# Gated cross-attention with experts: block 0's first chunks between the last attention turns, and the gate in two halves

## The reference, cut to what matters

```python
def reference(x, ctx_1024, mask_BxSxS2_bk1, g_xattn, g_ffn, ...):
    # x, ctx: (32, 128, 128) float32; 16 heads of 8; 8 experts, hidden width 512
    x = x + jnp.tanh(g_xattn[0]) * attention(_layernorm(x), ctx_1024, ctx_1024, mask, Wq, bq, ..., Wo, bo)
    x = x + jnp.tanh(g_ffn[0]) * ffn(_layernorm(x), Wg, bg, Wt, bt, W1, b1, W2, b2)
    return x

def ffn(inputs, ...):
    x = inputs.reshape(-1, 128)                        # 4096 tokens
    gate = jax.nn.softmax(x @ Wg + bg, axis=-1)        # 8 experts
    thr = jax.nn.sigmoid(x @ Wt + bt) * 0.125
    adapted = gate - thr
    w = adapted * (adapted >= 0)
    s = jnp.sum(w, axis=-1, keepdims=True)
    w = w / jnp.where(s == 0, 1, s)
    h = jax.nn.gelu(jnp.einsum('td,edf->etf', x, W1) + b1[:, None, :])   # every expert on every token
    eo = jnp.einsum('etf,efd->etd', h, W2) + b2[:, None, :]
    return jnp.einsum('te,etd->td', w, eo).reshape(inputs.shape)
```

## Time and profile before

| | us |
|---|---|
| three runs: median (lowest to highest) | 647.18 (643.64 to 647.93) |
| profiled execution: its own time | 640.58 |
| its span in the profile | 638.7 |
| TensorE busy in it | 596.9 |
| VectorE / ScalarE / POOL busy | 483.0 / 376.8 / 175.1 |
| mean granted clock of TensorE | 0.975 of full |

### The profile page before, as it was taken

One profiled execution on the slowest core, in us unless ns is written; L12 is line 12 of the kernel. 1 busy time (PEld: TensorE's weight loads), 2 busy tenths in 40 slices (PEclk: granted clock), 3 DMA queues, 4 the chain that ended last, 5 costly groups with the idle time before them and its releaser, 6 DMA issues.

```text
span 638.7 us, 13719 instructions
## 1 busy us (share of the span) xinstructions
PE 596.9 (93%) x4482; PEld 451.5 (71%) x4482; DVE 483.0 (76%) x926; ACT 376.8 (59%) x620; POOL 175.1 (27%) x223
## 2 busy tenths in 40 slices
PE   7688999999999986499999999999999999999998
PEld 5455666666666654478788788788787887887886
DVE  5467677777777764468888788888888888888886
ACT  2144555555555454277677667666676666666663
POOL 5433344544342331002212212112212112121121
PEclk9799899999999999599999999999999999999999
DMA  5955555656544510041121121121121121111210
GB/s 145 247 167 169 141 138 141 176 163 161 174 129 124 151 23 2 3 89 45 40 67 50 50 63 46 41 66 49 49 58 43 47 66 49 44 58 46 63 52 16
DMA packets 43966, 55.12 MB, mean 86 GB/s; under 512 B 9488, under 2 KB 27792, under 8 KB 42384
## 3 DMA queue, kind: packets, MB, share of 16 engines
q1 hardware_dynamic: 43472, 53.99, 30.2%
q10 hardware_dynamic: 448, 0.53, 0.3%
HBM read 39.16 MB, written 14.81 MB: 84 GB/s over the span
## 4 chain that ended last, share of the span: by engine, by line
PE 82%; DVE 5%; DMA 4%; ACT 4%; SPq 3%; issue 2%; ACTq 0%; POOL 0%; DVEq 0%
PE ps_h L1087 9%; PE ps_y L1067 9%; PE ps_y L1069 9%; PE ps_y L1068 9%; PE ps_h L1089 9%; PE ps_h L1088 9%; PE misc L931 4%; PE scores L869 4%; PE scores L897 3%; DMA kq_st<-maxT 3%; PE scores L909 3%; PE scores L886 3%; ACT probs L532 2%; PE misc L1035 1%; PE misc L957 1%
## 5 line engine op out<-in xcount | busy, mean ns | idle before, releaser
L616 ACT ACTIVATE h_sb<-ps_h,b_sb 128x512 f32<-128x512 f32 x256 | 176.2, 689 | 108.7 <-PE ps_h L1089 95.4
L820 DVE TENSOR_TENSOR h_low<-h_sb,h_high 128x512 fp32r<-128x512 f32 x256 | 164.3, 682 | 0.0
L495 POOL TENSOR_TENSOR yT<-yT,weighted 128x512 f32<-128x512 f32 x54 | 69.6, 1289 | 301.5 <-DVE weighted L808 301.5
L816 DVE CAST h_high<-h_sb 128x512 fp32r<-128x512 f32 x128 | 98.5, 770 | 68.1 <-ACT h_sb L616 68.1
L646 DVE TENSOR_REDUCE neg_max<-scores 128x8 f32<-128x1024 f32 x64 | 77.9, 1221 | 43.6 <-PE scores L869 43.6
L1087 PE MATMUL ps_h<-x_high,w_high 128*128 (+1 forms) x256 | 102.9, 402 | 1.7 <-ACT h_sb L616 1.7
L1067 PE MATMUL ps_y<-h_high,w_high 128*128 128x512 f32 x256 | 101.3, 396 | 0.6 <-DVE h_low L820 0.6
L1069 PE MATMUL ps_y<-h_high,w_low 128*128 128x512 f32 x256 | 101.2, 395 | 0.0
L1068 PE MATMUL ps_y<-h_low,w_high 128*128 128x512 f32 x256 | 101.2, 395 | 0.0
L1089 PE MATMUL ps_h<-x_high,w_low 128*128 (+1 forms) x256 | 100.8, 394 | 0.0
L1088 PE MATMUL ps_h<-x_low,w_high 128*128 (+1 forms) x256 | 100.3, 392 | 0.0
(11 more groups left out here) (124 smaller groups left out, 710.3 us busy)
## 6 DMA issues: line engine op xcount, KB each, us to landing
w_row<-w_scratch SPq DMA_DIRECT2D x64, 256.0 KB, 3.1
kq_st<-kq_scratch SPq DMA_DIRECT2D x64, 192.0 KB
kq_scratch<-kq_parts SPq DMA_DIRECT2D x30, 256.0 KB, 3.2
w_raw<-in_w_ffn SPq DMA_DIRECT2D x16, 256.0 KB, 3.3
kq_scratch<-kq_parts SPq DMA_DIRECT2D x32, 128.0 KB, 3.3
ctx_sb<-in_ctx SPq DMA_DIRECT2D x16, 128.0 KB, 2.6
out_y<-y_out SPq DMA_DIRECT2D x7, 256.0 KB, 2.3
x_all<-in_x SPq DMA_DIRECT2D x13, 128.0 KB, 2.2
```

What stands on the lines that cost most here:

```text
L616: nc.scalar.activation(h_sb[:, j % HBUF, :], ps_h[:, j % 4, :], ACT.Gelu_apprx_tanh, bias=b1_sb[:, j:j + 1]).then_inc(h_done, 1)
L816: V.tensor_copy(h_high[:, j % HBUF, :], h_sb[:, j % HBUF, :]).then_inc(high_odd, 1)
L820: V.tensor_tensor(h_low[:, j % HBUF, :], h_sb[:, j % HBUF, :], h_high[:, j % HBUF, :].bitcast(F32), ALU.subtract).then_inc(low2_done, 1)
```

## The change

It writes the same computation in another order.

- Block 0's chunks 0 to 7 (first halves) and 0 to 3 (second halves) go, on all three engines, between the steps of turns 16 to 19. The helpers `first`, `second`, `hidden`, `high`, `low` are taken out of the block bodies for it; block 0's body starts at chunk 8 (TensorE, ScalarE) or pair 6 (VectorE).
- ScalarE loads the Gelu table in turn 16 (`ready_gelu`, a Gelu of two columns), behind the last exponentials.
- The gate is split by tokens. Half 0 (blocks 0 to 3): steps 1 and 2, 3 to 7, 8 to 11, 12 to 15 stand behind the logits of turns 12, 13, 14 and 15 on VectorE, `gate_exps(0)` in turn 13 on ScalarE, `turn_gate(0)` in turn 17 on TensorE, `gate_copy(0)` in turn 17 on ScalarE. Half 1: steps inside block 1 of the expert stage, at pairs 0 and 2 one each, from pair 12 to 24 two each (the last has one), `gate_exps(1)` behind chunk 6, `turn_gate(1)` behind chunk 28, `gate_copy(1)` behind chunk 30. Each half is stored to DRAM by itself, the second behind block 1's loads of `w_row`.
- PSUM: `ps_y` changes places with `ps_t`, so that `ps_h` and `ps_y` lie over `scores` and only `ps_t` over `misc`; `expert_wT` goes to the end of the second stage's buffers.

TensorE, before: from the last turned maxima (`max_parts`, turn 15) to the first expert matmul. `x2n` is turned for x2T, `wg_sb` are logits, `ps_t<-ident_sb,g_exp` is the gate's turn.

The diff, cut to its core (waits and helpers as they are where not shown):

```diff
+            def gate_exps(half):
+                ts = slice(B // 2 * half, B // 2 * (half + 1))
+                act.wait_ge(g_dve, 15 * half + 2)
+                nc.scalar.activation(g_exp[:, ts, :], g_exp[:, ts, :], ACT.Exp).then_inc(g_act, 1)
+                nc.scalar.activation(g_thr[:, ts], logits[:, ts, E], ACT.Exp, scale=-1.0).then_inc(g_act, 1)
+            def ready_gelu():
+                act.wait_ge(tanh_done, 1)
+                nc.scalar.activation(spare[:], tanh_g[:], ACT.Gelu_apprx_tanh).then_inc(gelu_ready, 1)
+                wait_spare_loads(act)
+                act.wait_ge(wts_in, N_WTS)
...
@@ ScalarE, behind x2_high @@
+                    if g == NG - 2:
+                        hidden(0, 3)
+                        hidden(0, 4)
+                        gate_copy(0)
+                        hidden(0, 5)
+                        hidden(0, 6)
+                    elif g == NG - 1:
+                        hidden(0, 7)
...
@@ ScalarE, block bodies @@
+                    hidden(g, j)
+                    if isinstance(g, int) and g == 1:
+                        if j == 6:
+                            gate_exps(1)
+                        elif j == 30:
+                            gate_copy(1)
...
@@ VectorE, behind the logits @@
+                    if 8 <= g < 12:
+                        dve.wait_ge(misc_read[bank_of("gate")], fills("gate", NG // 2 - 1))
+                        gate_steps(0, ((1, 2), (3, 7), (8, 11), (12, 15))[g - 8])
+                    elif g == NG - 4:
+                        misc_wait_full(dve, "V1", NG - 1)
+                        low(0, 0)
+                    elif g == NG - 3:
+                        low(0, 4)
+                    elif g == NG - 2:
+                        high(0, 5)
+                        low(0, 5)
...
@@ VectorE, block bodies @@
+                    if isinstance(g, int) and g == 1:
+                        if j in (0, 2):
+                            gate_steps(1, (j // 2 + 1, j // 2 + 1))
+                        elif 12 <= j <= 24:
+                            gate_steps(1, (j - 9, min(j - 8, 15)))
...
@@ TensorE @@
+                    pe.wait_ge(x2n_done, g * GB + GB)
+                    if g == NG - 1:
+                        pe.wait_ge(g_copied, 1)
+                    turn("x2T", g, lambda b: x2n[:, u, b, :])
+                    if g == NG - 1:
+                        second(0, 3)
...
+                    if g == NG - 1:
+                        second(0, 1)
+                        misc_wait_read(pe, "x2T", NG - 2)
+                        turn_gate(0)
...
-            pe.wait_ge(g_dve, 15)
-            for q in range(2):
-                for k in range(4):
-                    tiles = g_exp[:, (4 * q + k) * TPB:(4 * q + k + 1) * TPB, :].rearrange("p t e -> p (t e)")
-                    ins = nc.tensor.transpose(ps_t[0:TPB * E, q, k, :], tiles, ident[:])
-                ins.then_inc(g_full, 1)
-            pe.wait_ge(wsplit_done, NW)
             pe.wait_ge(x2low_done, NG)
             pe.wait_ge(x2high_done, NG)
...
@@ SP @@
+            store_weights(0)
+            body_b(0)
+            body_b(1)
+            store_weights(1)
```

More of the change, by code:

```diff
@@ L587, in body @@
                     nc.scalar.activation(headsT[:, 1, :], misc[:, bank_of("V1"), 0:2 * P], ACT.Copy).then_inc(misc_read[bank_of("V1")], 1)
+                    if g == NG - 1:
+                        for j in range(3):
+                            hidden(0, j)
                 if (g := group_at(it, 3)) is not None:
@@ L597, in _, with body_b @@
             loop(body)
-            act.wait_ge(g_dve, 2)
-            nc.scalar.activation(g_exp[:], g_exp[:], ACT.Exp).then_inc(g_act, 1)
-            nc.scalar.activation(g_thr[:], logits[:, :, E], ACT.Exp, scale=-1.0).then_inc(g_act, 1)
-            for q in range(2):
[L604 to L623, removed]
+            def body_b(g, start=0):
+                for j in range(start, CH):
+                    hidden(g, j)
[4 more added lines that the diff above has]
+                            gate_copy(1)
+            body_b(0, 8)
+            body_b(1)
+            with act.Fori(2, NB) as g:
+                body_b(g)
         @block.vector
@@ L935, in body, with turn_gate @@
+            def turn_gate(half):
+                pe.wait_ge(g_dve, 15 * half + 15)
+                for k in range(4):
+                    tiles = g_exp[:, (4 * half + k) * TPB:(4 * half + k + 1) * TPB, :].rearrange("p t e -> p (t e)")
+                    ins = nc.tensor.transpose(ps_t[0:TPB * E, 1, k, :], tiles, ident[:])
+                ins.then_inc(g_full, 1)
             def body(it):
@@ L1000, in body @@
                     values(g, 1, u)
+                    if g == NG - 1:
+                        first(0, 2)
+                        first(0, 3)
                 if (g := group_at(it, 0)) is not None:
@@ L1028, in body @@
                     ins.then_inc(misc_full[bank_of("gate")], 1)
+                    if g == NG - 3:
+                        first(0, 6)
+                        second(0, 2)
+                        first(0, 7)
                 if (g := group_at(it, -1)) is not None:
@@ L1037, in body @@
                     ins.then_inc(misc_full[bank_of("heads")], 1)
+                    if g == NG - 1:
+                        first(0, 4)
+                        second(0, 0)
                 if (g := group_at(it, 0)) is not None:
@@ L1096, in body_b @@
                         untranspose(g - 1)
-            loop_b(pe, body_b)
+                    if isinstance(g, int) and g == 1 and j == 28:
+                        turn_gate(1)
+            body_b(0, 8)
+            body_b(1)
+            with pe.Fori(2, NB) as g:
+                body_b(g)
             def onto(what, halves, first, last):
```

205 lines of the change are left out of this document (135 added, 70 removed).

## The result

The changed kernel takes **622.14 us** (median of 4 runs, 620.89 to 624.14), the kernel before 645.41 in the same session (4 runs, 641.58 to 647.93): ratio 0.9647, 95% interval 0.9587 to 0.9708. In a later session it was 623.28 (6 runs) against 644.05 (11 runs), 0.9686 (0.9654 to 0.9719). Forecast were 632.7, with a range from 627.0: right in sign, 10.6 us too slow, and outside the range.

What follows compares the result with a forecast made beforehand. TensorE alone was taken to set the expert stage's pace, with a hole before it. Gain 17.6 - 2.2 - 0.85 = 14.5 us: 640.58 becomes 626.1 profiled, plus 6.6 gives 632.7; range 627 to 640.5.

Steps and rivals of the forecast that it cites:

- Moved buffers and banks: nothing: Second stage's buffers in SBUF and PSUM: claimed that their new places cost or gain nothing.
- T8: Instant when chunk 8 of block 0 starts on TensorE: 279.64 us before, forecast at 262.0.
- The 6.6 us between profile and median: Whole kernel: median of three runs, 647.18, lies 6.6 above the profiled 640.58; the same difference was added to 626.1.
- the hole: Stretch between attention and expert stage where TensorE falls to 6 and 4 tenths busy (240 to 272 us).
- 17.6 us to T8: Block 0's first eight chunks fill the attention's end, gate gone: chunk 8 starts 17.6 us earlier; bounds 15 and 19.
- 2.2 us in turns 12 to 15: Gate's first half on VectorE ahead of the reciprocal in the attention: costs 2.2 us; bounds 0.8 and 3.7.
- 0.85 us in block 1: Gate's second half in the expert stage: 0.4 us stall from table switches, 0.45 for TensorE's turns; bounds 0.45 and 4.
- A busy ScalarE: Rival, chance 0.15: three table switches cost up to 0.76 us more each, VectorE falls back 1 us; time 636.
- The clock did not fall: Rival, chance 0.12: TensorE's clock still halves between attention and chunk 8 of block 0; time 637.5.
- the steps meshed: Rival, chance 0.08, said the interleaving doesn't mesh: five hops of 0.7 us more in the in-order queues; time 636.
- the hole's rest: Rival, chance 0.03: without that rest a lower clock is granted through the whole expert stage; at 0.94, time 655.
- SP's store and load cost nothing: SP's queue: first gate store, then w_row issued at 263.5, first combine wanted at 266.4; 1 us spare, cost nothing.

## Why the forecast was wrong, by its own steps

The forecast was 640.58 - 14.5 = 626.1 for a profiled execution, and 6.6 more for the median. The profiled execution came out at 622.45, the median at 622.14.

**"Moved buffers and banks: nothing"** is the term of the sum that failed, and the forecast names no row for it. It is worth 4.7 us: behind T8 the changed kernel takes 355.92 us, and 360.67 with the 8 bytes of `spare` behind the buffers. With block 1's cost taken off, the stage is 3.1 us shorter than before, where the forecast had it unchanged to the microsecond. The banks and `expert_wT` do cost nothing.

**The 6.6 us between profile and median** is the second step that failed. It took three runs of before for typical; later sessions of 25, 7, 17 and 11 runs have medians of 644.24, 642.65, 643.71 and 644.05. So 640.58 is some 3.5 us under before's median, not 6.6. The range had the same fault: it allowed 3.5 us between runs, where the three runs already lay 4.3 apart and the 25 later ones 9.3. And the difference doesn't carry over: the changed kernel's profiled execution lies 0.3 above its median. What made before's fortunate run fortunate, an early end of the attention and a short way to T8, was partly in the hole, and the hole is gone: its way to T8 is 13.83 to 13.92 us in six profiles, where the old order gives 31.8 to 33.3. In medians, the start of 647.18 was 3.2 us too high, and the gain was 644.0 - 622.6 = 21.4 us where 14.5 were forecast.

**17.6 us to T8:** 18.0 in the two profiles, 18.9 against a typical execution of before. The walk by hops was right: the steps come in the order and at the distances forecast, to 0.5 us once both are counted from the end of the last masked scores, with ScalarE as the pole. Right too was that turning the weights falls off the path (0.60 us for four at 259.52, instead of 1.89 for eight at 267.01).

**2.2 us in turns 12 to 15:** 1.7 to 1.8, shown by the kernel that moves the steps. The half-width steps start 0.31, 0.29 and 0.21 us apart, as assumed (0.32, 0.28 and 0.20); the first of each turn begins before the logits have ended, and the four stretches of steps take 0.5, 1.3, 1.0 and 1.0 us instead of 0.6, 1.4, 1.1 and 1.1. In the first profile another 1.2 us was lost around the wait of 1.33 us, with the clock at 0.50 from 246 to 248 us. The changed kernel's second profile and three more kernels with the steps in this place have the same wait without that spell, so the loss belongs to the one execution. By its own signs the forecast had this as one of being wrong (a half clock); it lies ahead of the last masked scores and not in the hole.

**0.85 us in block 1:** 1.5 (46.11 us against 44.60 in the kernel before with the 8 bytes, whose matmuls have the same pitch). The chunk distances of the two differ in three places. Behind the switch it is 0.8 us: one chunk takes 1.96 instead of 1.37, with the wait of 0.33 and a wider matmul behind it, and two chunks later one takes 1.55 instead of 1.36. At the turns it is 0.5 (1.72 and 1.48 instead of 1.36 twice). Where the hardware loop begins it is 0.25: TensorE waits there for the last Gelu of block 1, and ScalarE's gate copy (342.46) stands ahead of it, so the wait is 0.53 us (343.84) instead of 0.29. Forecast were 0.4, 0.45 and nothing. VectorE kept its cover, though two of its steps met POOL's addition (1.33 and 1.29 us instead of 0.29 and 0.17), which I had not priced. The Trainium skill, "SBUF — State Buffer", section "Who interferes with whom", says that a VectorE instruction with two SBUF inputs contends with a GpSimd instruction that reads SBUF. These rows agree: each of the two begins under 0.15 us behind a POOL addition of 1.29 us and ends with it, to 0.2 us.

**The rivals.** A busy ScalarE pays for the load alone: 308.17 lies 0.02 us behind the previous Gelu's end, and the next activation starts 1.30 us later, twice. The drain of about 1380 ns that the Trainium skill, "ScalarE: Activation LUTs", "What ACT_TABLE_LOAD costs", adds to the load did not show here; the measurement decides. The 0.76 us of idle time in the earlier trace rows was a wait for TensorE. The clock did not fall between the last masked scores and T8 in any of the profiles of the new order, the steps meshed, and the expert stage kept 1.00 from the first slice to the last without the hole's rest. SP's store and load cost nothing, as forecast, but by other numbers: w_row is issued at 263.61 where 263.5 was forecast, and that agreement is luck. The last masked scores end 3.0 us later than the forecast counted from, and from the store's issue (260.98) to w_row's it takes 2.63 us, not the 4.8 of the earlier trace rows.

With the terms as measured, 18.9 - 1.8 - 1.5 + 4.7 = 20.3 us, from 644.0 it gives 623.7; the ten runs have 622.6. The rest of 1.1 us is no more than single executions vary by, from which the terms are read, and is not explained further.

## What to carry to other kernels

Fill the waits at the end of one stage with the first work of the next, and walk the busiest helper engine's queue instruction by instruction, since it sets the new end; the steps that are slipped into a full stage belong behind what the bounding engine waits for. Before a profile is used as a baseline, see how it stands to ten or more runs, and don't carry its offset over to a kernel in which the varying stretch is gone. A small tensor ahead of large buffers is a change of its own: take the distance of the matmuls in a steady stretch, before and after.

## What the runs showed of the hardware

- The place of a matmul's operand buffer in SBUF, by 8 bytes, changes the matmuls' pitch in a full stream: 877 instead of 864 in 200 us, at the same granted clock, 5.0 us over the 359 behind T8.
- Four of the six matmul distances of a chunk get longer by it, from 0.227 us to between 0.232 and 0.235: those behind the three matmuls that read `h_high` or `h_low`, and that behind the first that reads x. In the profile of before the second-half distances average 0.234 us where VectorE is busy all through and 0.232 where it is idle, 0.233 and 0.234 for ScalarE. So they don't follow what these engines do at that moment, and the mechanism stays open.
- In the changed kernel the mean distance of starts also rises from 0.227 to between 0.230 and 0.235 us from 310 to 317 us (waits left out), during and behind the table switch, and is 0.227 again from 318 us on. Why was not tested.
- A table load on a busy ScalarE costs 1.30 us from start to next activation.
